# Layer 0's attention: four heads in row and column groups of TensorE, with the next batch's projections between the heads

## What is computed

```python
h = jnp.concatenate([x, latents], axis=1)          # context 361 + own 100 tokens
q = (latents @ q_w + q_b).reshape(b, k_len, NH, DH)  # NH, DH = 16, 32
kv = (h @ kv_w + kv_b).reshape(b, p + k_len, NH, DH, 2)
kmat, v = (kv[..., 0], kv[..., 1])
attn = jnp.einsum('bkhd,bnhd->bhkn', q, kmat) / DH
attn = jnp.where(full_mask[:, None, None, :], attn, -jnp.inf)
attn = jax.nn.softmax(attn.astype(jnp.float32), axis=-1).astype(q.dtype)
attn_out = jnp.einsum('bhkn,bnhd->bkhd', attn, v).reshape(b, k_len, H)
attn_out = attn_out @ out_w + out_b + residual
```

## Time and profile before

| | us |
|---|---|
| median of 3 runs | 4331.4 (4328.82 to 4335.36) |
| span of the profiled execution | 4338.2 |
| layer 0's attention in it | 29 to 557 |

### The profile page before, as it was taken

One profiled execution on the slowest core, in us unless ns is written; L12 is line 12 of the kernel. 1 busy time (PEld: TensorE's weight loads), 2 busy tenths in 40 slices (PEclk: granted clock), 3 DMA queues, 4 the chain that ended last, 5 costly groups with the idle time before them and its releaser, 6 DMA issues. The chain is left out here.

```text
span 4338.2 us, 51209 instructions
## 1 busy us (share of the span) xinstructions
PE 3694.2 (85%) x17671; PEld 2781.4 (64%) x17671; DVE 1757.5 (41%) x3586; ACT 1221.5 (28%) x3084; POOL 559.9 (13%) x475
## 2 busy tenths in 40 slices
PE   4999979796658699999989789898989979688886
PEld 3777758453324487887878578787878867344442
DVE  2445442318873423323232422323232241566664
ACT  2344332111011123222222222222222232445452
POOL 0000020123430300000000100000000010432312
PEclk9999989899979799999999899999999989768688
DMA  2110120100000312222121132222122120110001
GB/s 85 48 46 25 37 77 15 38 10 3 0 10 29 106 42 78 74 59 80 41 73 46 38 109 55 84 55 84 41 78 55 27 80 10 61 38 27 31 2 31
DMA packets 142038, 209.09 MB, mean 48 GB/s; under 512 B 18915, under 2 KB 104357, under 8 KB 141933
## 3 DMA queue, kind: packets, MB, share of 16 engines
q0 software_dynamic: 67584, 94.64, 8.5%
q1 hardware_dynamic: 74348, 113.17, 8.5%
HBM read 191.04 MB, written 13.47 MB: 47 GB/s over the span
## 5 line engine op out<-in xcount | busy, mean ns | idle before, releaser
L63 PE MATMUL work<-cT_layer_hi,wk_layer_hi 128*128 128x362 f32 x1024 | 390.3, 381 | 0.0
L1908 ACT ACTIVATE p_layer<-scores,neg_max_layer 100x362 f32<-100x362 f32 x256 | 144.5, 565 | 740.4 <-DVE neg_max_layer L1963 739.1
L1944 DVE TENSOR_TENSOR values_layer<-work,value_bias_layer 121x512 f32<-121x512 f32 x192 | 132.4, 690 | 519.3 <-PE work L65 519.3
L64 PE MATMUL work<-cT_layer_lo,wk_layer_hi 128*128 128x362 f32 x1024 | 336.8, 329 | 0.0
L65 PE MATMUL work<-cT_layer_hi,wk_layer_lo 128*128 128x362 f32 x1024 | 336.6, 329 | 0.0
L63 PE MATMUL work<-wv_layer_hi,cT_layer_hi 128*121 128x512 f32 x768 | 311.9, 406 | 0.0
L64 PE MATMUL work<-wv_layer_lo,cT_layer_hi 128*121 128x512 f32 x768 | 303.1, 395 | 0.0
L65 PE MATMUL work<-wv_layer_hi,cT_layer_lo 128*121 128x512 f32 x768 | 302.6, 394 | 0.0
L1751 POOL DMA_DIRECT2D cT_layer_hi<-ctxT_hi x64 | 47.7, 745 | 1745.5 <-PE work L65 1743.3
L1890 ACT ACTIVATE keysT_layer<-work 128x361 f32<-128x361 f32 x256 | 120.7, 472 | 510.4 <-PE work L65 510.4
L1820 PE MATMUL o<-pT_layer,values_layer 121*128 121x100 f32 x1536 | 215.8, 276 | 56.9 <-ACT pT_layer L1914 56.9
(11 more groups left out here) (353 smaller groups left out, 7737.9 us busy)
## 6 DMA issues: line engine op xcount, KB each, us to landing
cT_layer_hi<-ctxT_hi POOLq DMA_DIRECT2D x64, 722.0 KB, 4.9
cT_layer_lo<-ctxT_lo POOLq DMA_DIRECT2D x64, 722.0 KB, 6.1
l0mlp_staged<-in_L_xattn_mlp_w_dram SPq DMA_DIRECT2D x16, 512.0 KB, 4.2
staged_layer<-in_L_xattn_wq_dram SPq DMA_DIRECT2D x8, 1024.0 KB, 5.2
staged_layer<-in_L_xattn_wk_dram SPq DMA_DIRECT2D x8, 1024.0 KB, 5.1
staged_layer<-in_L_xattn_wv_dram SPq DMA_DIRECT2D x8, 1024.0 KB, 5.1
staged_layer<-in_L_xattn_wo_dram SPq DMA_DIRECT2D x8, 1024.0 KB, 5.6
l2mlp_staged<-in_L_xattn_w_fc_dram SPq DMA_DIRECT2D x16, 512.0 KB, 4.1
```

What stands on the lines that cost most here:

```text
L63: pe.matmul(out, cut_a(a.hi), cut_b(b.hi), start=start, stop=False)
L64: pe.matmul(out, cut_a(a.hi), cut_b(b.lo), start=False, stop=False)
L1908: act.activation(probs[x % 4][:, 0:KEYS2], ps_scores[x % 2][0:L, 0:KEYS2], ACT.Exp, bias=neg_max[:, x:x + 1], accum_out=sums[:, x:x + 1]). ...
L1944: dve.tensor_tensor(values[c % 2][:, j, :], bank("v", c, j)[0:T2, :], value_bias[:, min(j, 1), :], ALU.add).then_inc(dve_copied, 1)
```

## The change

The hardware loop is gone; the program is written out for all 128 heads (a global count g over the batches, `HEADS` = 128).

- Scores: for each group of four heads (`QUAD0`) four matmuls follow each other. Head i uses rows 32i to 32i + 31 of `qT` and `keysT` as operands and writes bank i of four score banks. `q_heads` with its zeros is gone; `qT` is one copy with bias.
- VectorE does one fused operation a head (add the mask, negate, running minimum), ScalarE the exponential with scale -1, VectorE a reciprocal a head, and GpSimd scales the probabilities in place. `probs` and `probsT` have eight buffers (`RING`).
- The transposes of head g - 3 have one PSUM bank; ScalarE copies the even heads, VectorE the odd ones.
- Attend: for each group of four heads, 16 matmuls, with 32 value columns stationary and 100 probability columns moving, the four heads in the four column groups of one bank. The result has features on its rows, so a copy per batch by ScalarE writes `attT` directly. The transposes and copies of `layer0_output` are gone.
- The projections and transposes of the next batch are cut into 40 units and spread over the 16 heads of the current one (`order`, `slots`); their tiles share two PSUM banks. The token transposes in them are a batch further ahead. Keys, queries and values have two buffers each.
- Loads: tokens of batch 0 first, one token buffer and one mask buffer instead of two; the mask of the next batch is waited for ahead of the context's store.

```diff
-        hcat = [sb(f"hcat{s}", [T0, NT0, D]) for s in range(2)]
+        hcat = sb("hcat", [T0, NT0, D])
...
-        work = [own.enter_context(nc.psum_tensor(f"work{i}", [P, 512], F32)) for i in range(3)]
+        work = [own.enter_context(nc.psum_tensor(f"work{i}", [P, 512], F32)) for i in range(BANKS)]
...
+    order = ["q", ("k", 0), ("t", 0), ("k", 1), ("k", 2), ("t", 1), ("k", 3), ("v", 0), ("t", 2),
+             ("v", 1), ("v", 2), ("t", 3), ("v", 3)]
...
+    slots = {}
+    for b in range(B - 1):
+        units = units_of(b + 1)
+        for n, unit in enumerate(units):
+            slots.setdefault(b * H0 + n * H0 // len(units), []).append(unit)
...
+            for h in range(HEADS):
+                pool.wait_ge(inverted, h + 1)
+                p, column_ = probs[h % RING], h % (2 * H0)
+                pool.tensor_scalar(p[:], p[:], inverse[:, column_:column_ + 1], 1.0, ALU.mult, ALU.mult
+                                   ).then_inc(scaled, 1)
...
+            def scores(b, m):
+                s, h = b % 2, b * H0 + m * QUAD0
+                pe.wait_ge(q_copied, b + 1)
+                pe.wait_ge(keys_copied, KT * b + m + 1)
+                for i in range(QUAD0):
+                    if h + i >= QUAD0:
+                        pe.wait_ge(shifted, h + i - QUAD0 + 1)
+                    rows = slice(DH0 * i, DH0 * (i + 1))
+                    pe.matmul(ps_scores[i][0:L, 0:N0], qT[s][rows, m, :], keysT[s][rows, m, :], start=True, stop=True
+                              ).then_inc(scored, 1)
...
+            def attend(b, m):
+                h = b * H0 + m * QUAD0
...
+                wait_probsT(pe, h + QUAD0 - 1)
+                for j in range(NT0):
+                    for i in range(QUAD0):
+                        head = m * QUAD0 + i
+                        mm = pe.matmul(ps_att[DH0 * i:DH0 * (i + 1), m * L:(m + 1) * L],
+                                       values[b % 2][:, j, head * DH0:(head + 1) * DH0], probsT[(h + i) % RING][:, j, :],
+                                       start=(j == 0), stop=(j == NT0 - 1))
+                mm.then_inc(attended, 1)
+
+            for u in first:
+                unit(*u)
+            for g in range(HEADS + ATTEND):
+                if g < HEADS and g % QUAD0 == 0:
+                    scores(g // H0, g % H0 // QUAD0)
+                units = slots.get(g, [])
+                for u in units[:1]:
+                    unit(*u)
+                if 0 <= g - TURN < HEADS:
+                    turn(g - TURN)
+                for u in units[1:]:
+                    unit(*u)
+                h = g - ATTEND
+                if h >= 0 and h % QUAD0 == QUAD0 - 1:
+                    attend(h // H0, h % H0 // QUAD0)
...
+                if g < HEADS:
+                    dve.wait_ge(scored, g + 1)
+                    if g >= RING:
+                        dve.wait_ge(turned, g - RING + 1)
...
+                    dve.tensor_tensor_reduce(probs[g % RING][:], ps_scores[g % QUAD0][0:L, 0:N0], mask_add[b % 2][:],
+                                             -1.0, 3e38, ALU.add, ALU.min, neg_max[:, column_:column_ + 1]
+                                             ).then_inc(shifted, 1)
+                if 1 <= g <= HEADS:
+                    invert(g - 1)
+                h = g - TURN
+                if 0 <= h < HEADS and h % 2 == 1:
+                    copy_probsT(h)
+                for kind, b, j, n, steps in slots.get(g, []):
+                    if n == steps - 1:
+                        evacuate(kind, b, j)
...
-            turn_tokens(pe, k, tiles, "attT", k.ATT, lambda b: None)
             pe.wait_ge(loaded, 48)
-            project_tokens(pe, tiles, "out", attT, out_w, KT,
-                           lambda b: tiles.wait_out(pe, "attT", range((b // 4) * KT, (b // 4 + 1) * KT)))
+            project_tokens(pe, tiles, "out", attT, out_w, KT)
```

More of the change, by code:

```diff
@@ L207, in _, with layer0_attention, units_of @@
             last.then_inc(turned, 1)
-def layer0_attention(nc, k, ins, ctx):
+def layer0_attention(nc, k, ins, ctx, attT):
     x, context, mask = ins["x"], ins["ctx_2048"], ins["mask_BxS2_ik0"]
     k.ctxT = {part: nc.dram_tensor(f"ctxT_{part}", [B, P, KT, S], F32R, kind="Internal").ap() for part in ("hi", "lo")}
+    QUAD0 = 4
+    QUADS = H0 // QUAD0
+    RING = 8
+    TURN, ATTEND = 3, 4
+    HEADS = B * H0
+    order = ["q", ("k", 0), ("t", 0), ("k", 1), ("k", 2), ("t", 1), ("k", 3), ("v", 0), ("t", 2),
+             ("v", 1), ("v", 2), ("t", 3), ("v", 3)]
+    def units_of(batch):
+        out = []
+        for tile in order:
+            kind, j = ("q", 0) if tile == "q" else tile
+            of = batch + 1 if kind == "t" else batch
+            if of < B:
+                steps = 1 if kind == "t" else KT
+                out += [(kind, of, j, n, steps) for n in range(steps)]
+        return out
+    first = [("t", 0, t, 0, 1) for t in range(KT)] + units_of(0)
+    slots = {}
[3 more added lines that the diff above has]
+            slots.setdefault(b * H0 + n * H0 // len(units), []).append(unit)
+    started = [u[:3] for u in first + [u for g in sorted(slots) for u in slots[g]] if u[3] == 0]
+    BANKS = 2
+    number = {tile: n for n, tile in enumerate(started)}
     def sem(name):
@@ L233, in layer0_attention @@
         values_w = Split(own, nc, "values_w", [P, KT, D])
-        keysT = sb("keysT", [P, KT, N0])
+        keysT = [sb(f"keysT{s}", [P, KT, N0]) for s in range(2)]
         keys_bias = sb("keys_bias", [P, KT])
[L236 to L241, removed]
@@ L242, in layer0_attention @@
[L242 to L247 removed]
+        values = [sb(f"values{s}", [T0, NT0, D]) for s in range(2)]
+        qT = [sb(f"qT{s}", [P, KT, L]) for s in range(2)]
@@ new lines, in layer0_attention @@
+        probs = [sb(f"probs{i}", [L, N0]) for i in range(RING)]
+        probsT = [sb(f"probsT{i}", [T0, NT0, L]) for i in range(RING)]
+        neg_max = sb("neg_max", [L, 2 * H0])
+        sums = sb("sums", [L, 2 * H0])
+        inverse = sb("inverse0", [L, 2 * H0])
+        work = [own.enter_context(nc.psum_tensor(f"work{i}", [P, 512], F32)) for i in range(BANKS)]
+        ps_scores = [own.enter_context(nc.psum_tensor(f"scores{i}", [P, 512], F32)) for i in range(QUAD0)]
+        ps_probsT = own.enter_context(nc.psum_tensor("turned", [P, 512], F32))
@@ L286, in bank_of, with bank, wait_evacuated @@
[L286 to L294, removed]
+        def bank(kind, b, j):
+            return work[number[kind, b, j] % BANKS]
+        def wait_evacuated(eng, kind, b, j):
+            if kind == "t":
+                eng.wait_ge(rest_done, KT * b + j + 1)
+            elif kind == "q":
+                eng.wait_ge(q_copied, b + 1)
+            elif kind == "k":
+                eng.wait_ge(keys_copied, KT * b + j + 1)
+            else:
+                eng.wait_ge(values_copied, NT0 * b + j + 1)
@@ L332, in _ @@
+            for s in range(2):
+                sp.wait_ge(ctxT_stored[s], 32 * (B // 2))
         @block.gpsimd
@@ new lines, in _ @@
+            last.then_inc(prepared, 1)
+            for t in range(KT):
+                for n, w in enumerate((keys_w, values_w)):
+                    dve.wait_ge(w_rounded, 2 * t + n + 1)
+                    w.rest(dve, lambda y: y[:, t, :], kv_w[t % 2][:, n:2 * D:2]).then_inc(w_split, 1)
+                evacuate("t", 0, t)
+            dve.wait_ge(weights_loaded, 16)
+            for kind, b, j, n, steps in first[KT:]:
+                if n == steps - 1:
+                    evacuate(kind, b, j)
```

406 lines of the change are left out of this document (191 added, 215 removed).

## The result

The changed kernel takes 4206.3 us (median of 4 runs, 4189.1 to 4216.3) against 4330.4 us for the kernel before: ratio 0.971, 95% interval 0.968 to 0.974. I had forecast 4265 (4205 to 4350). The time is within the range, by 1.3 us at its lower end, but it is the time of rival A (4209), not of the forecast.

What follows compares the result with a forecast made beforehand. TensorE was taken to bound layer 0's attention: start 92.7 + seven windows of 52.8 + last batch 28 = 490.3 us instead of 556.9, so 66.6 us off the median 4331.4 gives 4265 us, range 4205 to 4350.

Steps and rivals of the forecast that it cites:

- rival A: Scores and attend: all four groups run at once, passes included; window 45.0 us, 4209 us in all; chance 0.18.
- Scores, 2.1 us a group: Four heads' score matmuls on TensorE: partly overlapped, five slots of 0.42 us instead of eight, 8.4 us a window.
- the second pass of a head can only overlap the first pass of the next: Scores: float32 passes start in program order, so a group takes five slots instead of eight, 2.1 us.
- Attend, 1.9 us: Attend's 32 entries a group on TensorE: taken between 1.35 us paired and 2.6, making 7.6 us a window.
- Changes of grouping, 0.1 us each: TensorE switching between row or column groupings, four times a group: 1.6 us a window, bounds 0 and 0.35 each.
- Projections, 27.9 us: Next batch's q, keys, values and token transposes in a window: 5.2 + 10.2 + 11.1 + 1.4 us, instructions unchanged.
- Bank waits, 1.0 us: Two work banks instead of three: tiles of keys or values wait for copies, 1.0 us a window.
- VectorE, ScalarE, GpSimd at nothing: Other engines in a window: VectorE and ScalarE some 23 us each, GpSimd's scaling hidden; no cost.
- Tokens of batch 2, 2 us: SyncE's queue at the start: tokens issued at about 93, needed at about 101 us; 2 us once (0 to 6).
- Last batch, 28 us: Last batch without projections between heads: 4 x 5.8 us of TensorE + 5 for the pipeline's end.
- Output stage: After attention: loses 32 transposes, but they ran while its weights loaded; that wait stays, so nothing is gained.
- B: Scores and attend: no overlap at all; window 61.0 us, last batch 36.5, 4331 us, no change; chance 0.19.
- C: Slower granted clock in the attention: at 0.76 a window takes 68.6 us, 4375 us in all; chance 0.18.

Runs made afterwards that it cites:

- e1: Changed kernel with all four heads' score matmuls on rows 0 to 31 instead of four row groups: 4339.4 us, ratio 1.004 to the kernel before.
- e8: Changed kernel with attend's two loops swapped, one head's four matmuls following each other on its own column group: 4239.6 us, ratio 0.978 to the kernel before.
- e2: Changed kernel with all four heads' attend writing partitions 0 to 31, head by head: 4270.7 us, ratio 0.989 to the kernel before.
- e5: Changed kernel with the scaling of the probabilities on VectorE instead of GpSimd: 4214.3 us, ratio 0.973 to the kernel before.
- e6: Changed kernel with VectorE building batch 0's mask ahead of the copies of batch 0's projections: 4197.2 us, ratio 0.968 to the kernel before.
- e3: Changed kernel with scores on one row group and attend on one column group, projections still between heads: 4371.3 us, ratio 1.012 to the kernel before.
- e4: Changed kernel with the next batch's projections in one block at a batch's fifth head instead of spread: 4366.1 us, ratio 1.012 to the kernel before.
- e10: Kernel of e6 with three extra matmuls of unread results ahead of each head of the last batch: 4177.9 us, ratio 0.967 to the kernel before.

## Why the prediction was right in the time and wrong in the mechanism

The balance, by the parts of my sum: start of the scores 90.0 instead of 92.7 (2 us of it were the wait for tokens, which came in the first window); seven windows 305.2 instead of 369.6 us (54.9 for the first, with the wait; five of 42.4; 38.5 for the one without new tokens); the last batch 40.2 instead of 28. 435.3 against 490.3.

That the time lies within the range is luck. The range reaches down to rival A, and two errors of the other sign, the wait and the last batch, held the time up: had they cost what I gave them, the attention would end some 22.7 us earlier, and by the same reckoning the time would be about 4187 us, below the range.

- **Scores, 2.1 us a group: wrong.** It measured 0.97, with its change of grouping. The step that failed is "the second pass of a head can only overlap the first pass of the next": the serial price was right (3.35 in e1), the slots were two, not five. The first passes of the four heads run at once, and then the second ones; that starts follow the program, on which the pairing rested, is what e8 speaks against. Of the 10.4 us by which a window is shorter than forecast, 4.5 are here. Rival A's 0.95, and the 3.07 times of the Trainium skill (TensorE: Matmul & The Clock Gate, Part 3) that I weighed (1.1 us), were near it; from e1, (207.44 − 204.15) / 0.97 = 3.4 times.
- **Attend, 1.9 us: wrong for the same reason, and for a second.** It measured 0.82, 0.026 us an entry. I took the 0.08 us that no entry had gone below as perhaps the price of issue. It isn't: four entries on four groups start 0.007 us apart, and on one group the distance is 0.086. It was also misread: in the kernel before, the second entry of a head's attend starts 0.033 us after the first in 104 of the heads. 4.3 us a window. The serial price, 2.7, measured 2.86 (e2).
- **Changes of grouping, 0.1 us each: right in size, one too many, and counted twice.** The first score entry starts 0.18 us after the last of attend, whose rounds are 0.086 apart; a dense entry starts 0.48 us after the last of the scores, where a stream is 0.39; and attend starts 0.30 after the last of the keys, which are 0.21 apart. That is 0.09 us each, three times a group. Two of them are inside the 0.97 and 0.82 and the third in the projections, so as a term of its own the 1.6 us a window are too much.
- **Projections, 27.9 us: near in sum (28.8 without waits), for two errors that nearly cancel.** q takes 3.65 instead of 5.2. But keys, values and the transposes of tokens take 25.2 without waits, not 22.7. Most of it is that each time that keys or values resume after another kind of entry, some 20 times a window, the first is 0.29 to 0.33 us from the next where the others are 0.21 (keys) or 0.23 (values) apart. A part comes back in the transposes of the probabilities, 5.2 us instead of 5.6: their last entry is 0.03 us from the dense one behind it instead of 0.09.
- **Bank waits, 1.0 us: right** (7.2 us in seven windows). **VectorE, ScalarE, GpSimd at nothing: right** in the steady state; the scaling takes 0.656 us, near the lower bound (0.53), and e5 shows its cover. In the last batch it was wrong: there TensorE waits 5.9 us for the scaling and 5.5 us for the single bank's copies, the two waits that I had named as signs of being wrong.
- **Tokens of batch 2, 2 us: wrong,** outside its bounds (0 to 6). The queue was named, the landing wasn't worked out: 4.8 us of issues and 10.4 us for the tokens' packets. The clock was also at 0.50 from 101.4 to 115.1 us; together the first window is 12.5 us longer than the others, and the seven windows of e6 are 13.0 us shorter.
- **Last batch, 28 us: wrong by 12.** I summed each engine's work at the full clock. What I left out is that one bank makes transposes and copies follow one another (4.3 us at the full clock, 7.4 at the low one), that they also wait for the scaling, and that in the pauses the clock falls to 0.50 (6.6 us with one bank); with both mended it takes 30.6 us.
- **Output stage: right.** Its weights are asked for at 435.59 and the first matmul starts at 443.26, 7.67 us later; before it was 7.73.
- **Rivals.** A was the case, but its end of 434.2 is so near to 435.3 by errors that cancel: start 2.7 and seven windows 9.8 us too long, last batch 13.7 too short. B is what e3 ran; its window was near (61.0 against 61.3 to 64.6), its last batch 26.7 us too short. C fell for the change as it is, but it was the right fear for e1 (0.88) and for the last batch (0.50 to 0.83 in the windows shown), which lose much of their time to the clock. In e4 (0.66 between the blocks) its share isn't known.

## What to carry to other kernels

Small matmuls in row and column groups do run at once, in float32 too (all first passes, then all second ones), if neighbours in the program use different groups: here 3.4 and 3.5 times faster, and less than half of attend's gain was left when a group's matmuls stood together. Packed attention heads are short for TensorE and have a long chain through the other engines, so here they paid only between dense work that keeps TensorE busy; sum the part that has none (here the last batch) by its chain and at the lower clock. And when a wait is put ahead of a queue's other transfers, work out when the last of them lands, not when it is issued.

## What was unexpected of the hardware

- The granted clock fell in stages where TensorE was busy 98%, and packing alone doesn't decide it. With both packed it was 1.00 after the wait for tokens; with the scores on one row group 0.88 (e1); with attend on one column group 1.00 (e2); with neither packed 0.95 (e3). I can't say from these runs what makes them differ.
- Matmuls start in another order than the program has them: the first passes of four heads' float32 scores, 0.007 us apart, and 0.45 us later the four second ones; and in e8 entries of the next head between those of a head that isn't through.
- Useless matmuls made a stage faster: three of 464 columns a head took the clock from 0.50 to 1.00 and 6.6 us off the last batch (e10).
- An entry of 116 x 32 by 100 columns costs 0.026 us in four column groups, 0.060 when a head's entries stand together, 0.089 in one group.
